# A three-layer attention chain: position rows on POOL's queue, earlier transposes, and half of the softmax pair sums added by a DMA

## The reference, cut to what matters

```python
# layers 0, 1, 2: self-attention over the 1024 positions, 8 heads of 16, 32, 32 channels
q, k, v = projections(x or group_norm(x))
s = scale * q @ k.T                       # per head, 1024 x 1024
s = s + pos[:, None] + pos[None, :]       # layer 0 only: a position bias for queries and for keys
p = exp(s - max(s)) / sum(exp(s - max(s)))
x = norm_or_residual(x, project(p @ v))
# layer 3: a gated channel attention without an N x N matrix
```

## Time and profile before

| | |
|---|---|
| median of 3 runs | 530.08 us (529.44 to 531.9) |
| profiled execution | 528.11 us, its span 526.4 us |
| mean granted clock of PE | 0.976 |
| busy: PE, DVE, ACT, POOL | 93%, 69%, 51%, 35% of the span |
| steps of layers 0, 1, 2 | about 32 to 148, 204 to 327 and 366 to 490 us |

### The profile page before, as it was taken

How to read it: one execution, slowest core, us unless ns; L and a number is a source line. 1 busy time by engine, 2 the same in 40 slices (tenths; PEclk the granted TensorE clock), 3 DMA queues, 4 the chain that set the end, 5 groups by cost and what they waited for, 6 DMA issues and landing times.

```text
span 526.4 us, 7243 instructions
## 1 busy us (share of the span) xinstructions
PE 488.2 (93%) x2388; PEld 249.3 (47%) x2388; DVE 361.9 (69%) x687; ACT 268.4 (51%) x522; POOL 186.0 (35%) x161
## 2 busy tenths in 40 slices
PE   8798989999889898899999999999799999999996
PEld 6455444444325764544444432655444444442463
DVE  7598766879245648887798832748697788872573
ACT  3137656657632432766666663041686665765032
POOL 8200000000000001686677783000486768767000
PEclk9869989999999998999999999999999999999999
DMA  4320432000000044133500000024305410000002
GB/s 142 58 55 17 132 54 42 2 2 2 2 0 0 1 114 96 32 109 77 134 35 2 0 2 2 0 57 104 81 6 126 97 36 2 2 1 1 0 1 80
DMA packets 12100, 22.46 MB, mean 43 GB/s; under 512 B 4390, under 2 KB 5550, under 8 KB 11936
## 3 DMA queue, kind: packets, MB, share of 16 engines
q1 hardware_dynamic: 11472, 21.77, 17.2%
q0 software_dynamic: 448, 0.22, 0.3%
q10 hardware_dynamic: 144, 0.02, 0.0%
HBM read 4.76 MB, written 1.05 MB: 11 GB/s over the span
## 4 chain that ended last, share of the span: by engine, by line
PE 60%; DVE 21%; SPq 9%; issue 4%; DMA 3%; ACT 2%; POOL 0%; ACTq 0%; DVEq 0%; POOLq 0%
PE PV L898 16%; DVE max L635 14%; PE S L887 12%; PE S L860 10%; SPq L281 5%; PE M L915 5%; PE S L1003 4%; DVE rec_sb L665 2%; SPq L288 2%; PE S L1048 1%; PE S L843 1%; PE PV L836 1%; PE M L836 1%; SPq L308 1%; DVE mHL L648 1%
## 5 line engine op out<-in xcount | busy, mean ns | idle before, releaser
L635 DVE TENSOR_REDUCE max<-S 128x1 f32<-128x512 f32 x384 | 244.5, 673 | 69.5 <-PE S L860 69.2
L487 ACT ACTIVATE E<-S 128x512 f32<-128x512 f32 x384 | 207.6, 600 | 115.6 <-PE S L887 112.6
L429 POOL TENSOR_TENSOR SUMS<-E 128x512 f32<-128x512 f32 x126 | 159.9, 1282 | 164.5 <-ACT E L487 163.4
L860 PE MATMUL S<-k_stack,q_stack 126*128 126x512 f32 x384 | 176.0, 469 | 5.5 <-DVE max L635 2.7
L887 PE MATMUL S<-q_stack,k_stack 128*128 128x512 f32 x384 | 164.0, 434 | 17.8 <-ACT E L487 6.2
L860 PEld LDWEIGHTS S<-k_stack,q_stack 126*128 126x128 f32 x384 | 75.4, 196 | 85.7 <-DVE max L635 52.2
L887 PEld LDWEIGHTS S<-q_stack,k_stack 128*128 128x128 f32 x384 | 73.6, 193 | 72.5 <-ACT E L487 27.0
L898 PE MATMUL PV<-E,V 128*32 128x512 f32 x768 | 95.8, 599 | 0.6 <-ACT pv_sb L494 0.6
L412 POOL TENSOR_TENSOR att<-pv_sb,rec_sb 128x512 f32<-128x512 f32 x9 | 11.5, 1277 | 132.2 <-DVE rec_sb L665 132.1
L665 DVE RECIPROCAL rec_sb<-den_sb 128x64 f32<-128x64 f32 (+1 forms) x54 | 35.9, 669 | 27.6 <-ACT den_sb L504 27.6
L898 PEld LDWEIGHTS PV<-E,V 128*32 128x32 f32 x768 | 20.2, 109 | 46.0 <-issue 30.6
(11 more groups left out here) (175 smaller groups left out, 301.3 us busy)
## 6 DMA issues: line engine op xcount, KB each, us to landing
k_stack<-kH SPq DMA_DIRECT2D x32, 128.0 KB, 2.3
q_stack<-qH SPq DMA_DIRECT2D x40, 64.0 KB, 2.0
k_stack<-kL SPq DMA_DIRECT2D x16, 128.0 KB, 2.3
q_stack<-qH SPq DMA_DIRECT2D x16, 128.0 KB, 2.3
q_stack<-mHL SPq DMA_DIRECT2D x96, 2.0 KB
q_stack<-qL SPq DMA_DIRECT2D x20, 64.0 KB, 2.0
X<-x_in_dram SPq DMA_DIRECT2D x2, 512.0 KB, 5.5
k_stack<-kH SPq DMA_DIRECT2D x16, 64.0 KB, 2.5
```

Source lines behind the costliest of these rows:

```text
L429: pool.tensor_tensor(SUMS[:, slot, :], E[:, E_PLAN[s][0], :], E[:, E_PLAN[s + 1][0], :], ALU.add).then_inc(sum_ready, 1)
L487: act.activation(E[:, slot, :], B[:, ring_of_scores(s) % B_RING, :], ACT.Exp, scale=1.0 if l == 0 else float(HEAD_DIM[l]) ** -0.5).then_in ...
L635: dve.tensor_reduce(max8[:, m % 2, r:r + 1], A[:, n % A_RING, :], AX.X, ALU.max, negate=True).then_inc(a_used, 1)
L860: pe.matmul(A[:, n % A_RING, :], q_stack[0:SHIFT_ROW, slot, q0:q0 + P], k_stack[0:SHIFT_ROW, slot, k0:k0 + HALF], start=True, stop=True).t ...
```

## The change

It has three parts.

1. `load_pos` moves from SP to POOL, ahead of POOL's layer 0 multiplications, with a semaphore of its own for each head (`pos_late`). PE waits for it before the head's first `scores_for_max`. `stack_count` no longer counts the position rows.
2. `transpose_max` stands ahead of `scores_for_max` in its step instead of behind it.
3. In layers 1 and 2 POOL still makes the four pair sums of a unit, but then issues a DMA that adds sums 2 and 3 onto sums 0 and 1 (128 partitions by 1024 elements, 512 KB). `denominators` has two groups for each block, at steps 41 and 49 after the block's start. The last unit has no such DMA: its third pair sum and its last two exponential tiles are three extra products in column group 3 behind the last group. Slots 0 to 11 of `SUMS` hold kept sums of six units, 12 to 15 the added ones of two. ACT waits on `pv_done` and `sum_ready` for a used slot of `E`.

```diff
@@ sync
                 for h in range(4, NH):
                     if h >= SLOTS:
                         sp.wait_ge(b_done, STEPS * l + 32 + TILES * (h - SLOTS + 1))
-                        if l == 0:
-                            load_pos(h)
                     load_q(sp, l, h, both, stack_dma[h])
@@ gpsimd
+            def load_pos(h):
+                pool.wait_ge(b_done, 32 + TILES * (h - SLOTS + 1))
+                for part, src in enumerate((posH, posL)):
+                    for dst, r in ((q_stack, p0 + 2 + part), (k_stack, p0 + part)):
+                        pool.dma_start(dst[r:r + 1, slot_of(h), :].bitcast(F32), src[h:h + 1, :]).then_inc(pos_late[h - SLOTS], 16)
...
                 if l == 0:
+                    for h in range(SLOTS, NH):
+                        load_pos(h)
                     for b in range(BLOCKS - 1):
                         normalise(l, b)
...
-                        slot, freed = SUM_PLAN[j, k]
+                        slot = sum_slot(j, k)
                         pool.wait_ge(e_ready, STEPS * l + s + 2)
-                        if freed:
-                            pool.wait_ge(den_done, PAIRS_L * (l - 1) + freed)
+                        if k < 2 and j >= SUM_UNITS:
+                            pool.wait_ge(den_done, DENS_L * (l - 1) + 2 * ((j - SUM_UNITS) // HEADS_B) + k + 1)
...
+                        elif k == 2 and j >= 2:
+                            pool.wait_ge(sum_dma[j % 2], dma_count(l, j - 2))
...
                         pool.tensor_tensor(SUMS[:, slot, :], E[:, E_PLAN[s][0], :], E[:, E_PLAN[s + 1][0], :],
                                            ALU.add).then_inc(sum_ready, 1)
+                    if j < UNITS_L - 1:
+                        pool.wait_ge(sum_ready, sum_count(l, j, PAIRS - 1))
+                        kept, added = sum_slot(j, 0), sum_slot(j, 2)
+                        pool.dma_start(SUMS[:, kept:kept + 2, :], SUMS[:, added:added + 2, :],
+                                       accum_op=ALU.add).then_inc(sum_dma[j % 2], 16)
                     if j in (9, 13):
                         normalise(l, (j - 9) // 4)
@@ scalar, probabilities
-                if freed and l == 0:
-                    act.wait_ge(pv_done, freed)
-                elif freed:
-                    act.wait_ge(den_done, PAIRS_L * (l - 1) + freed)
+                if freed:
+                    act.wait_ge(pv_done, PAIRS_L * l + freed)
+                if freed and l:
+                    b, k = (freed - 1) // PAIRS, (freed - 1) % PAIRS
+                    act.wait_ge(sum_ready, sum_count(l, HEADS_B * (b + 1) - 1, k))
@@ tensor, denominators
-                pe.wait_ge(sum_ready, sum_count(l, 4 * b + 3, k))
...
+                first = HEADS_B * b
+                folded = HEADS_B if b < BLOCKS - 1 else HEADS_B - 1
+                pe.wait_ge(sum_dma[0], dma_count(l, first + 2))
+                pe.wait_ge(sum_dma[1], dma_count(l, first + folded - (2 if folded < HEADS_B else 1)))
+                if folded < HEADS_B:
+                    pe.wait_ge(sum_ready, sum_count(l, UNITS_L - 1, k + 1))
+                for u in range(HEADS_B):
+                    mm = pe.matmul(M[DP * u:DP * (u + 1), :], ones[:, 0:DP], SUMS[:, sum_slot(first + u, k), :], start=(k == 0),
+                                   stop=(k == 1 and u < folded))
+                if k and folded < HEADS_B:
                     pe.wait_ge(e_ready, STEPS * (l + 1))
+                    for i, rhs in enumerate((SUMS[:, sum_slot(UNITS_L - 1, 2), :], E[:, E_PLAN[STEPS - 2][0], :],
+                                             E[:, E_PLAN[STEPS - 1][0], :])):
+                        mm = pe.matmul(M[DP * folded:, :], ones[:, 0:DP], rhs, start=False, stop=(i == 2))
                 mm.then_inc(den_done, 1)
@@ tensor, the loop
                 for s in range(-LEAD, STEPS):
+                    if -ROWS_STEP <= s < STEPS - ROWS_STEP and (s + ROWS_STEP) % TILES == 0:
+                        transpose_max(l, (s + ROWS_STEP) // TILES)
                     if s + LEAD < STEPS:
                         scores_for_max(l, s + LEAD)
-                    if -ROWS_STEP <= s < STEPS - ROWS_STEP and (s + ROWS_STEP) % TILES == 0:
-                        transpose_max(l, (s + ROWS_STEP) // TILES)
...
-                        if phase == 4 and l:
-                            denominators(l, b, k)
+                        if phase == 4 and k in (1, 2) and l:
+                            denominators(l, b, k - 1)
...
                 for t in range(5, TILES):
-                    if l:
-                        denominators(l, BLOCKS - 1, t - 4)
+                    if t == TILES - 1 and l:
+                        denominators(l, BLOCKS - 1, 1)
                     values(l, BLOCKS - 1, t)
```

More of the change, by code:

```diff
@@ L30 @@
 E_SLOTS = 34
-SUM_SLOTS = 16
+SUM_UNITS = 6
+SUM_SLOTS = 2 * SUM_UNITS + 4
 SLOTS = 5
@@ L66, in slot_plan, with sum_slot @@
     return plan
[L69 to L78, removed]
+def sum_slot(j, k):
+    return 2 * (j % SUM_UNITS) + k if k < 2 else 2 * SUM_UNITS + 2 * (j % 2) + k - 2
 def attention_chain(nc, x, w0, w1, w2, w3, pos_bias, cols, row3, out):
@@ L171, in attention_chain @@
         pool_chain, dve_chain = sem("pool_chain"), sem("dve_chain")
+        pos_late = [sem(f"pos_late{i}") for i in range(NH - SLOTS)]
         pos_ready, pos_rows, one_rows_in = sem("pos_ready"), sem("pos_rows"), sem("one_rows_in")
@@ L182, in attention_chain @@
         sum_ready, den_done, pv_done = sem("sum_ready"), sem("den_done"), sem("pv_done")
+        sum_dma = [sem(f"sum_dma{i}") for i in range(2)]
         pv_out, gathered, den_out = sem("pv_out"), sem("gathered"), sem("den_out")
@@ L221, in proj_bank, with stack_count @@
             return (B[:, 0, :], B[:, 1, :], PV[:, :], M[:, :])[n] if n < 4 else (PV[:, :], M[:, :])[n % 2]
[L223 to L227, removed]
+        def stack_count(l):
+            return 16 * 6 * (l + 1)
         def second_count(l):
@@ L233, in slot_of, with dma_count @@
             return h % SLOTS
-        E_PLAN, SUM_PLAN = slot_plan(), sum_plan()
+        E_PLAN = slot_plan()
+        DENS_L = 2 * BLOCKS
         PAIRS_L = BLOCKS * PAIRS
         SUMS_L = UNITS_L * PAIRS - 1
+        def dma_count(l, j):
+            return 16 * ((UNITS_L // 2 - j % 2) * (l - 1) + j // 2 + 1)
         def sum_count(l, j, k):
@@ L310, in shift_rows @@
                                  mHL[:, m % 2, r, :].bitcast(F32)).then_inc(shift_dma[m % 2], 16)
[L312 to L316, removed]
             first, second, both = slice(0, HALF), slice(HALF, N), slice(0, N)
@@ L424, in _ @@
                         s = TILES * j + 2 * k
-                        slot, freed = SUM_PLAN[j, k]
+                        slot = sum_slot(j, k)
                         pool.wait_ge(e_ready, STEPS * l + s + 2)
-                        if freed:
-                            pool.wait_ge(den_done, PAIRS_L * (l - 1) + freed)
+                        if k < 2 and j >= SUM_UNITS:
+                            pool.wait_ge(den_done, DENS_L * (l - 1) + 2 * ((j - SUM_UNITS) // HEADS_B) + k + 1)
+                        elif k < 2 and l > 1:
+                            pool.wait_ge(den_done, DENS_L * (l - 1))
+                        elif k == 2 and j >= 2:
+                            pool.wait_ge(sum_dma[j % 2], dma_count(l, j - 2))
+                        elif k == 2 and l > 1:
+                            pool.wait_ge(den_done, DENS_L * (l - 1))
                         pool.tensor_tensor(SUMS[:, slot, :], E[:, E_PLAN[s][0], :], E[:, E_PLAN[s + 1][0], :],
                                            ALU.add).then_inc(sum_ready, 1)
+                    if j < UNITS_L - 1:
[3 more added lines that the diff above has]
+                                       accum_op=ALU.add).then_inc(sum_dma[j % 2], 16)
                     if j in (9, 13):
@@ L460, in project_out @@
                     for h in range(HEADS_B):
-                        act.wait_ge(stack_dma[h], stack_count(l, h))
+                        act.wait_ge(stack_dma[h], stack_count(l))
                         if kind == "q":
@@ L500, in denominators_out @@
                 else:
-                    act.wait_ge(den_done, PAIRS_L * (l - 1) + PAIRS * (b + 1))
+                    act.wait_ge(den_done, DENS_L * (l - 1) + 2 * (b + 1))
                 if l + b:
@@ L553, in _ @@
             act.wait_ge(sum_ready, SUMS_L * 2)
-            act.wait_ge(den_done, PAIRS_L * 2)
+            act.wait_ge(den_done, DENS_L * 2)
             act.activation(XT[:, :, C:C + 1], ones[:, 0:TILES].rearrange("p (t o) -> p t o", o=1), ACT.Copy).then_inc(xt_used, 1)
@@ L661, in reciprocals @@
                     else:
-                        dve.wait_ge(den_done, PAIRS_L * l)
+                        dve.wait_ge(den_done, DENS_L * l)
                     if b == 0 and l:
@@ L853, in scores_for_max @@
                 if r == 0:
-                    pe.wait_ge(stack_dma[h], stack_count(l, h))
```

(13 more changed lines are left out.)

## The result

The changed kernel takes 536.93 us (median of 4 runs) against 529.76 us for the kernel before. The ratio is 1.0135, 95% interval 1.0106 to 1.0164: slower by 7.2 us, where 3.0 us less was forecast. The profiled execution took 538.2 us with a span of 536.5.

A forecast was written before the change was run, and what follows sets the result against it. PE was taken as the main bound (60% of the chain of waits), but not everywhere. Position rows -3.4, groups -3.2, DMA waits +3.0, small things +0.6 gave -3.0 us: 527.1 us from 530.08, range 523 to 535.

The forecast's parts named there:

- Position rows: Layer 0: with position rows off SP's queue, PE's wait for the shift rows goes; three units take 21.73 us, -3.4 us.
- The margin of 0.1 us: Layer 0, step 48: shift rows land at 71.1, PE wants them at about 71.2, so the wait just goes.
- rival two: A draw: the sum DMA takes 6.1 us (530.1), or head 5's shift rows stay late (530.5); chance 0.20.
- Removed groups: Layers 1 and 2: 8 of 16 denominator groups a layer go, gaining 1.6 us a layer, 3.2 for both.
- The naive 16 us: Layers 1 and 2, PE the only bound: each removed group gains its full 1.0 us; total 514.3 us, chance 0.01.
- The tail: Behind a layer's loop: two more groups go but nothing is gained, column group 3 has seven products either way.
- The DMA's landing and the wait for it: Layers 1 and 2: sum DMA lands in 5.3 us, issue 1.1; PE waits 1.5 us a layer.
- the 3.0 us of waits: PE's waits for the sum DMA, both layers: 0.1 to 0.2 us at step 41, 1.3 at step 126, each layer.
- rival one: The sum DMA is in time everywhere, landing in 4.2 us or less: -6.0, so 524.1 us; chance 0.19.
- The shift rows of three units in each layer have little slack behind the stack transfers, and the sum DMA is in flight beside them: 0.2 a layer: Layers 1 and 2, small things: these shift rows beside the sum DMA add 0.2 us a layer.
- Rival three: Slower: the adding DMA takes 7.0 us, its issue 1.5, PE's waits 16.0 in all: +10.0, so 540.1; chance 0.18.

The follow-up runs named there:

- after_3q: The changed kernel with sum DMAs of three quarters of the size (384 of 512 columns of each slot added): 529.46 us, ratio 0.9989 to the kernel before.
- the trace of the copy: The changed kernel with a plain copy of the same 512 KB in place of the accumulating DMA: 524.71 us, ratio 0.9914 to the kernel before.
- after_split: The changed kernel with two sum DMAs of 256 KB for each unit, behind the third and fourth pair sum: 544.93 us, ratio 1.0319 to the kernel before.

## Why the prediction was wrong

- **Position rows: right in size.** 25.09 us for three units became 21.73. Forecast -3.4; the two measurements of part 1 alone give -3.3 and -3.9 by their ratios. The margin of 0.1 us was read too small: the 1.64 us of the earlier trace rows start with the second issue, not with its end, so the rows land at some 70.5 and the margin is 0.7 us. The branch of rival two that hung on it was less likely than it looked.
- **Removed groups: right in place, too high in size.** Units of 6.81 to 6.83 us at steps 29, 53 and 85 in the kernel without the DMA, 7.22 at 61 and 93. But the layers got shorter by 1.0 and 0.9 us there, not by 1.6 each. With part 1 the forecast was -6.6 before any cost, measured -5.8. The naive 16 us never appeared.
- **The tail: right.** From the group at step 126 to the layer's last `values` product are 8.5 us before and after.
- **The DMA's landing and the wait for it: too high, and for the rest hidden.** 4.7 us instead of 5.3, issue 0.88 instead of 1.1. Of the 3.0 us of waits that I summed at most the 0.39 us shown above came. That was not only the landing. At the group at step 126 of layer 1 PE came at 325.33, 4.5 us later than before, held up by the shift rows, and the last packet of unit 14's DMA had ended at 324.77. In after_3q, where PE is less held up, a DMA that lands in 4.4 us makes it wait 1.9 us: 0.49 at step 41 and 0.70 and 0.67 at step 126. So some of this wait would probably come back once the shift rows were in time. The Trainium skill has 2.0 us plus the bytes over 436 GB/s (DMA: Bandwidth & Descriptors, on the anatomy of one DMA on the SWDGE path), an estimate of 3.2 us for a plain copy; the trace of the copy has 3.1. With the two source reads of the Trainium skill (Collectives: The Full Stack, on the bandwidth ceiling) the estimate was 4.4 us; the add took 4.7. Both are over the 4.2 us up to which rival one holds, so that estimate did not lead to rival one alone.
- **"The shift rows of three units in each layer have little slack behind the stack transfers, and the sum DMA is in flight beside them: 0.2 a layer": this step failed.** It was 6.1 and 6.4 us a layer. Each half of it was at hand. The trace before gives a slack of 1.0 to 1.3 us for the three units meant, and 0.6 for unit 3, which stands behind no stack transfer. The burst could have been worked out as well: reads of 1024 KB over 16 engines, at the pace that I used for the landing, are some 3 us on each engine (an estimate). A shift row behind it on the same engine is late by up to that. I thought only of who waits for the new DMA, not of who shares its engines, and took three units into the sum; in layers 1 and 2 the rows of 26 of 32 units were more than 0.7 us late, and ten became waits, two of them with a lower clock behind them.
- **Rival three** had the sign and a size in its neighbourhood, but another mechanism, a late sum DMA. In the changed kernel PE lost at most 0.39 us to it. The same terms with 12.5 in place of 0.4 for the two layers, and 0 in place of 3.0, give -6.6 + 12.5 + 0.2 = +6.1, against +7.2 measured.

What stays open: the span between layers 0 and 1 was 1.8 us longer in the profile after, with a longer stretch at the lower clock (165.0 to 175.2 us). It was so in the profiles of some other kernels without the DMA as well and not of all, so I don't count it as an effect.

## What to carry to other kernels

A transfer that nobody waits for is not free: look up which small transfers with a deadline run on the same DMA engines, and compare their slack with the new burst's time on one engine, not with its share of the span. The cost sets in where the delay passes the slack, so it doesn't shrink in proportion: here a DMA of half the bytes, with two thirds of the engine time, cost a quarter. And a late transfer can hide another: the wait for the sums showed only in a kernel whose shift rows were less late. Before work is taken off the busiest engine, compare two stretches that differ by just that work: here 1.0 us of PE was worth 0.46 or 0.05.

## What was not expected of the hardware

- An accumulating DMA keeps an engine busy 339 ns for each 4 KB packet (median), a copy 160 ns. Smaller accumulated packets are not cheaper in proportion: 187 ns for 2 KB (after_split), 149 for 1.5 KB, 112 for 1 KB.
- The delay reached not only the flight of the small transfers but also SP's issue of them: 0.57 us alone, up to 1.6 us beside the bursts, though SP's queue and POOL's are different ones. Why is open.
